# Turning all four tiles of a far pair by DMA instead of two on TensorE

## What is computed

```python
Wh = h @ W.T
sim = Wh @ Wh.T / (norms * norms.T + EPS)
mask = (adj > 0) | eye
alpha = softmax(where(mask, sim, -inf), axis=1)
x = layernorm(x + alpha @ Wh)
agg = mask2 @ x / max(deg, 1)                 # mask2 = adj > 0
y = relu(concat([x @ W_self + b_self, agg @ W_nb + b_nb]) @ W_comb + b_comb)
out = layernorm(x + y)
```

## Time and profile before

| | us |
|---|---|
| median of 3 runs (lowest, highest) | 878.36 (876.25, 879.7) |
| the profiled execution, its own time | 876.79 |
| its span in the profile | 875.0 |
| PE busy / DVE busy / ACT busy in the span | 855.9 / 585.5 / 374.8 |

### The profile page before, as it was taken

The page is one execution under the profiler, slowest core; times in us unless marked ns, Lnnn a source line. Parts: engine busy times, 40 slices in busy tenths (PEclk is TensorE's granted clock), DMA queues, the critical chain, the costliest instruction groups (busy, mean ns, idle before and its releaser), DMA issues.

```text
span 875.0 us, 18251 instructions
## 1 busy us (share of the span) xinstructions
PE 855.9 (98%) x6871; PEld 685.3 (78%) x6871; DVE 585.5 (67%) x1336; ACT 374.8 (43%) x619; POOL 66.5 (8%) x177
## 2 busy tenths in 40 slices
PE   8999999999999999999999999989999999999997
PEld 6867777777777777777777777768888888888886
DVE  2777887879767797778878878889525333333333
ACT  4867656656556565555656556554210000000000
POOL 2400000000000000000000000011101110001101
PEclk9999999999999999999999999999999999999999
DMA  7997685567777777798879699865753303321300
GB/s 201 276 218 193 178 220 151 151 169 209 188 175 213 206 206 191 179 229 209 209 201 232 181 221 318 207 173 140 201 89 133 115 19 109 115 87 47 115 19 19
DMA packets 209566, 146.89 MB, mean 168 GB/s; under 512 B 123473, under 2 KB 187234, under 8 KB 208450
## 3 DMA queue, kind: packets, MB, share of 16 engines
q1 hardware_dynamic: 209282, 145.28, 62.1%
q0 software_dynamic: 192, 0.41, 0.2%
HBM read 95.83 MB, written 28.85 MB: 142 GB/s over the span
## 4 chain that ended last, share of the span: by engine, by line
issue 81%; PE 10%; POOL 5%; DVE 2%; ACT 1%; POOLq 1%; DMA 0%; DVEq 0%; SPq 0%; ACTq 0%
PE ps L1355 3%; POOL rstd L656 3%; POOL var_eps L654 2%; PE ps L1446 1%; PE ps L1448 1%; PE ps L1447 1%; PE ps L1386 1%; PE ps L1388 1%; PE ps L1387 1%; ACT mask L724 1%; PE ps L1440 1%; DMA feat<-xT 0%; ACT prob_hi L719 0%; DVE feat L873 0%; DVE work L1025 0%
## 5 line engine op out<-in xcount | busy, mean ns | idle before, releaser
L1446 PE MATMUL ps<-feat,prob_hi 128*128 128x257 f16 x1024 | 280.7, 274 | 4.0 <-DVE prob_lo L1032 3.9
L1448 PE MATMUL ps<-feat,prob_lo 128*128 128x257 f16 x1024 | 279.7, 273 | 0.0
L1447 PE MATMUL ps<-feat,prob_hi 128*128 128x256 f16 x1024 | 278.7, 272 | 0.0
L1635 PE MATMUL ps<-big,mgroup 128*128 128x257 f16 x992 | 219.2, 273 | 0.0
L1636 PE MATMUL ps<-big,mgroup 128*128 128x256 f16 x992 | 219.2, 273 | 0.0
L719 ACT ACTIVATE prob_hi<-work 128x512 f16<-128x512 f32 x172 | 106.6, 628 | 104.4 <-DVE work L992 42.1
L1032 DVE SCALAR_TENSOR_TENSOR prob_lo<-work,prob_hi 128x512 f16<-128x512 f32 x172 | 117.2, 686 | 22.6 <-ACT prob_hi L719 20.9
L1446 PEld LDWEIGHTS ps<-feat,prob_hi 128*128 128x128 f16 x1024 | 99.8, 97 | 30.3 <-DVE prob_lo L1032 5.4
L1447 PEld LDWEIGHTS ps<-feat,prob_hi 128*128 128x128 f16 x1024 | 100.4, 98 | 24.7
L712 ACT ACTIVATE work<-ps 128x512 f32<-128x512 f32 (+2 forms) x144 | 79.2, 552 | 74.2 <-PE ps L1388 70.7
L1448 PEld LDWEIGHTS ps<-feat,prob_lo 128*128 128x128 f16 x1024 | 99.5, 97 | 13.4
(11 more groups left out here) (142 smaller groups left out, 995.6 us busy)
## 6 DMA issues: line engine op xcount, KB each, us to landing
adj_sb<-adjT SPq DMA_DIRECT2D x128, 512.0 KB, 4.5
mask_spill<-mask SPq DMA_DIRECT2D x128, 128.0 KB, 4.0
mgroup<-mask_spill SPq DMA_DIRECT2D x8, 2048.0 KB, 8.0
xres<-x SPq DMA_DIRECT2D x8, 512.0 KB, 5.8
x1h_dram<-big SPq DMA_DIRECT2D x16, 256.0 KB, 5.5
out<-rows SPq DMA_DIRECT2D x32, 128.0 KB, 1.7
feat<-xT SPq DMA_DIRECT2D x7, 512.0 KB, 6.8
unit_dram<-feat SPq DMA_DIRECT2D x7, 512.0 KB, 4.5
```

What stands on the lines that cost most here:

```text
L1446: pe.matmul(acc(D + 1), prob_hi[:, s, cols], feat_hi_of(g)[:, r, 0:D + 1], start=start, stop=False)
L1447: pe.matmul(acc(D), prob_hi[:, s, cols], feat_lo_of(g)[:, r, :], start=False, stop=False)
L1448: return pe.matmul(acc(D + 1), prob_lo[:, s, cols], feat_hi_of(g)[:, r, 0:D + 1], start=False, stop=stop)
L1635: pe.matmul(agg_ps(q, D + 1), lhsT, z_hi_of(g)[:, r, 0:D + 1], start=(jb == 0), stop=False)
```

## The change

For far pairs, all four tiles are turned by DMA. `block_scores` and its eight transposes per pair go, and with them `mask_blocks`, `mask_direct`, `heads` and `tails` in far pairs: every tile now takes the way of `far_parts`. The two transposing loads of a pair are 512 KB each. In SP's order they stand inside the pair whose tiles they turn (after its second mask store) and no longer at the end of the pair before. The turned tiles are no longer stored as half-width strips: the adjacency and the masks of the turned side are loaded and stored in the direct shape. The buffers move into `mgroup[:, 1]`, so that the second group's masks are loaded later. The first group's masks are loaded at step 6 instead of 4. `unitT` and `x1T` are loaded by transposing DMAs straight from SBUF; the DRAM buffers go. The layout of `unitT` becomes block by block, so the moving operand of the score matmuls is four runs of 128 columns.

```diff
-MGROUP0_STEP = 4
+MGROUP0_STEP = 6
@@ SP
             def turn_far(a, b):
                 k = far_before(a) + b - a - 1
-                sync.wait_ge(far_hi_ready, 2 * (k + 1))
-                sync.wait_ge(far_lo_ready, 2 * (k + 1))
+                sync.wait_ge(far_hi_ready, GB * (k + 1))
+                sync.wait_ge(far_lo_ready, GB * (k + 1))
                 for h in range(2):
-                    sync.dma_start_transpose(far_turned(h).rearrange("p r (s i) -> p (r s) i", s=GB),
+                    sync.dma_start_transpose(far_turned[:, h].rearrange("p r (s i) -> p (r s) i", s=GB),
                                              far_parts[:, h].rearrange("p r i -> p (r i)")).then_inc(far_loaded, 16)
             def pair_far(a, b):
                 for m in range(4):
...
-                        store_turned(a, b, 3 - m, slot)
-                if b < G - 1:
-                    turn_far(a, b + 1)
+                        store_direct(b, a, m - 2, slot)
+                    if m == 1:
+                        turn_far(a, b)
-            def store_x1(a):
+            def turn_x1(a):
                 sync.wait_ge(x1_ready, (a + 1) * GB)
                 for h in range(2):
+                    sync.dma_start_transpose(x1T_of(a, h).rearrange("p b k i -> p (b k) i"), x1_half_of(a, h)).then_inc(x1T_loaded[a], 16)
@@ ACT, pair_far
                 def high(r):
                     act.wait_ge(exp_ready, f0 + r + 1)
                     wait(act, far_loaded, 32 * k)
...
-                for r in range(2):
-                    exponentials(t0 + r, c0 + r, f0 + r, r, GB)
+                for r in range(GB):
+                    exponentials(t0 + r, c0 + r, f0 + r, r, GB, 0, GB * (k - 1) + r + 1 if n else None)
                     high(r)
-                unit_kept(u0, 0, 2 * k + 1)
+                    if r in (1, 2):
+                        unit_kept(u0 + r - 1, r - 1, 4 * k + r)
...
@@ DVE, pair_far
+                for r in range(GB):
+                    if r % 2 == 0:
+                        keep_unit(r // 2)
                     damping(a, b * GB + r, c0 + r, f0 + r, r)
...
+                    low(r)
+                    if n:
+                        block_copied(b - 1, r, t0 - GB + r)
+                    masked_parts(t0 + r, r, kept(r // 2)[:, r % 2 * GW:(r % 2 + 1) * GW], far_parts[:, 0, r, :], far_parts[:, 1, r, :], lambda ap: ap)
+                    beside()
+                keep_unit(2)
+                keep_unit(3)
...
                 dve.wait_ge(far_loaded, 32 * (k + 1))
+                for x in range(GB):
+                    masked_parts(t0 + GB + x, x, kept_block(x), halved(far_turned[:, 0, x]), halved(far_turned[:, 1, x]), halved)
+                    beside()
@@ PE
-            def block_scores(r, f):
-                pe.wait_ge(exp_ready, f + 1)
-                for x in range(GB):
-                    ins = pe.transpose(score_ps(r)[:, x * P:(x + 1) * P], expo[:, r, x * P:(x + 1) * P], ident[:, :])
-                ins.then_inc(score_done, 1)
             def pair_far(a, b):
                 for j in range(STEP_TILES):
-                    if j < 2:
-                        front_far(a, b, GB + j)
-                    elif j >= GB and b < G - 1:
+                    if j >= GB and b < G - 1:
                         front_far(a, b + 1, j - GB)
```

More of the change, by code:

```diff
@@ L206, in gnn_program, with kept, kept_block @@
         mixw = rows
[L207 to L216, removed]
+        def kept(m):
+            return prob[:, m, :].bitcast(F16)
+        def kept_block(x):
+            return work[:, 6 * GW:8 * GW].bitcast(F16).rearrange("p (s i) -> p s i", s=GB)[:, :, x * P:(x + 1) * P]
         def halved(ap):
@@ L454, in _ @@
             load_unit(0, 1, 1, 3)
[L455 to L459, removed]
+            for g in range(1, PROMPT - 1):
+                turn_units(g)
             def load_norms(a):
@@ L709, in exponentials @@
                 wait_apart(act, score_done, c + 1, act_passed)
-                wait(act, prob_ready, t - since + 1)
+                if free is None:
+                    wait(act, prob_ready, t - since + 1)
+                else:
+                    act.wait_ge(far_lo_ready, free)
                 act.activation(expo[:, r, first:], score_ps(r)[:, first:], ACT.Exp,
@@ L1149, in pair_far, with beside @@
                 t0, f0, u0 = (first + more for first, more in zip(tiles_before(a), (GB + n * STEP_TILES, GB + n * GB, 2 + n * 4)))
-                c0 = scores_before(a) + GB + n * 6
-                h0 = heads_before(a) + GB + n * GB
+                c0 = scores_before(a) + GB + n * GB
                 k = far_before(a) + n
-                loaded = lambda m: 16 * ((u0 + m) // 4 + 1)
+                share = -(-len(between) // (G - b))
+                places = iter(range(1, STEP_TILES + 2))
+                def beside():
+                    place = next(places)
+                    for _ in range(place * share // (STEP_TILES + 1) - (place - 1) * share // (STEP_TILES + 1)):
+                        if between:
+                            between.pop(0)()
@@ L1159, in low @@
                                              op0=ALU.mult, op1=ALU.subtract).then_inc(far_lo_ready, 1)
-                def beside(count=1):
-                    for _ in range(count if between else 0):
-                        if between:
-                            between.pop(0)()
-                more = 2 if a == G - 2 else 1
-                for r in range(2):
-                    damping(a, b * GB + r, c0 + r, f0 + r, r)
-                low(0)
-                low(1)
-                keep(u0, 0, t0)
```

243 lines of the change are left out of this document (85 added, 158 removed).

## The result

| | median us | lowest, highest | over before |
|---|---|---|---|
| before | 878.68 | 876.25, 879.70 | |
| after | 942.47 | 940.94, 944.01 | 1.073 [1.0701, 1.0759] |

The change makes the kernel 7.3% slower. The forecast was 934 with a range of 897 to 960.

What follows compares the result with a forecast made beforehand. PE, busy for 98% of rows 1 to 6, was taken to bound the kernel. 876.8 - 21 (work removed) + 64 (waits for turned tiles) + 14 (VectorE's loop) = 934 us, range 897 to 960.

Steps and rivals of the forecast that it cites:

- transposes removed: PE, rows 1 to 6: 168 transposes in 42 groups of 0.43 us go, 18.1 us less.
- PE's small waits before, gone: Idle time of PE or its weight load ahead of the transposes, 6.8 us in all; 3 taken as saved.
- waits for the turned tiles: PE stands in each far pair of rows 1 to 6 until both transposing loads land: 64 us in sum.
- VectorE's loop: VectorE's work from landing to landing, 17.7 us against PE's 18.1; norm work on it adds 14 us, 0 to 30.
- clock behind the waits: Rival: PE's idle gaps bring 1.2 GHz back, 11 x 2.6 = 29 us, time 961, chance 0.08; not in the sum.
- T: Time for both 512 KB transposing loads of a far pair: 7.3 us taken, range 6 to 8.
- the chain: From the end of a pair's fourth tile's scores through exp, parts, loads and first masked tile: 2.9 + 7.3 = 10.2 us.
- The first rival: Transposing loads cost their issue, not their bytes: 4.5 us for both, wait hidden, time 867, chance 0.08.
- The second: Rival: transposing loads run at the plain rate, 4.8 us for both, time 880, no change to tell, chance 0.06.
- The cover: PE's other work while the turned tiles come: 7.9 us in middle pairs, 6.6 in first and last, 5.3 in row 6.
- The other edits: Direct-shaped loads and stores, `unitT` and `x1T` without DRAM, four-run score operands: costed at nothing.
- The signs that the forecast named: Stage of rows 1 to 6 470 to 480 us, PE busy around 395, 21 low-part waits, loads issued in 2.5 us.

Runs made afterwards that it cites:

- third experiment: All norm pieces of a far pair put at one place, just ahead of VectorE's wait for the landing, against the changed kernel: 941.5 us, 1.0714 of before.
- PE's work put back: Eight transposes with unused results added to every far pair, against the kernel that turns each pair's tiles in two halves: 870.76 us, 0.992 of before.
- two steps: Changed kernel with each pair's tiles 0 and 1 loaded as soon as ready, tiles 2 and 3 after, four 256 KB loads: 860.47 us, 0.9803 of before.

## Why the prediction was nearly right, step by step

The stage sum in the forecast's own terms, in us:

| step | forecast | measured |
|---|---|---|
| transposes removed | -18 | -18.1 |
| PE's small waits before, gone | -3 | -10 |
| waits for the turned tiles | +64 | +66.6 |
| VectorE's loop | +14 | 0 |
| clock behind the waits | 0 | +27.0 |
| sum | +57 | +65.5 |

**Removed: right for the work, too small for the waits.** The 21 waits for turned tiles make 66.6 of the 68.1 us of idle time, so 1.5 is left of the 11.5 that stood there before, and 10 went with the change, not 3. I had read the 6.8 us ahead of L1474 and missed the other small waits of the stage. That they go because PE's long stand in each pair gives everything else slack is my reading; no run shows it.

**T and the chain: right.** 7.3 taken, 6.85 measured in the pair shown and 7.2 in the mean of all; the chain 10.2 taken, 9.7 measured in the pair shown. Both ways to T in the forecast (four small loads in a row, and bytes at 210 GB/s) held: the new loads flow at 205 to 214 GB/s with the DMA share at 1.12 to 1.14. The first rival, a cost for each load and not for its size, would have had T at 4.5; it is refuted by 6.85, and by the 2.3 us of issue for 512 KB against 1.3 for 256 KB. The second, transposes at the plain rate, is refuted by the same 6.85 and by the 205 to 214 GB/s. By the Trainium skill ("Advanced Engine Details and Errata", X-Bar Transpose) T would have been 4.8 (the prediction's estimate from its 350 to 400 GB/s). The traces here do not agree with it, at 6.85.

**The cover: right, pair by pair.**

| pairs | forecast, each | measured, mean (lowest to highest) |
|---|---|---|
| 10 middle ones | 2.3 | 2.5 (2.0 to 3.3) |
| 5 first ones of a row | 3.6 | 3.6 (3.4 to 4.4) |
| 5 last ones | 3.6 | 3.7 (3.3 to 4.4) |
| row 6 | 4.9 | 5.2 |

**VectorE's loop: wrong.** This is the step where I took 14 of 0 to 30. Moving all of the pieces to where VectorE stands idle (third experiment) changed the time by 1 us, inside the noise. VectorE's loop was counted at 17.7 us and PE's at 18.1, and I took near equality as a cost. Why it was none is argued from the trace and not tried: the chain to the loads starts with PE's scores, for which ScalarE waits (198.1 us in 103 places), so the pieces ahead of it lie mostly in time that PE's order leaves free.

**The clock: this is the step that failed by most.** It stood among the rivals with 0.08 and not in the sum. The forecast itself had PE standing for 3.6 to 5 us in eleven places, and the only ground for no loss was that PE kept 1.00 before, when its longest wait in the stretch was 1.4 us. That says nothing of what long waits do. Measured were 27.0 us, against the rival's 29, but made up in another way: not eleven waits by 2.6 but sixteen by 1.4 to 2.9. In order of length, the 21 waits and what the matmuls behind them took too long:

```
wait  2.00 2.01 2.02 2.02 | 2.31 2.51 2.74 3.06 3.08 3.30 3.33 3.33 3.35 3.36 3.36 3.38 3.53 3.98 4.35 4.37 5.22
slow  0    0    0    0    | 1.7  1.7  1.4  1.7  1.7  1.6  0    1.6  1.5  1.4  1.6  1.7  1.7  1.7  2.9  1.7  1.6
```

Each costs less than the 2.6 of the rival because the clock is back before the block and the score tile are done: in the windows above, 0.50, then 0.77, then 1.00. The Trainium skill ("TensorE: Matmul & The Clock Gate", Why this matters for your kernels; the prediction names the section otherwise) warned of just this, that idle gaps between bursts of matmuls bring the lower clock back. The trace agrees: 16 of the 17 longer waits are followed by it.

**The two errors offset.** 14 too much for VectorE and 7 too little for small waits gone are 21 too much; 27 for the clock and 2.6 for longer waits are about 30 missing. Together 8.5, the distance from 934 to 942.5. The sum was nearer than its terms: that 934 lies within 1% of the result is luck, that PE would stand in each of the 21 pairs, and for how long, is not. Two sums of the rivals were off by 2 us without bearing on the forecast: 934 + 29 is 963 and not 961, and the second rival's 13 + 10 is 23 and not 25.

**The other edits: not nothing.** They were costed at 0. With PE's work put back, two steps are 6.6 us faster than before, so these edits and the new order of VectorE's work give some us. In the changed kernel itself this can't be seen behind the long waits.

**The signs that the forecast named** came as told where the chain was concerned: 21 waits for the low part, the loads issued in 2.3 us (2.5 told) with the second landing after 4.7 (4.6 told), no transposes. The stage was to last 470 to 480 us and lasted 485. PE busy was to be 395 and is 420.8: less the 27.0 of slow matmuls that is 394. VectorE's wait for the landing is there, but under the name "issue".

## What to carry to other kernels

Before work is moved from a busy engine to DMA, the whole way from the last input to the first use has to be set against the work that the busy engine has in that time; here 9.7 us against the 7.9 counted decided, not the 18 us of work saved. A batch of loads waits for its last member: the same bytes in two steps turned +7.3% into -2.0%. Where a forecast makes TensorE stand for long, again and again (here 16 of 17 waits of 2.3 us and more were followed by the lower clock, and none of the four of 2.0), the clock belongs in the sum. A mean clock under 1.00 in a windows' row, or a busy time that rises though work was taken away, was the sign of it here (0.94, and 7.7 us more).

## What was unexpected of the hardware

- The granted clock fell to 0.50 behind waits of only 2.3 to 2.7 us, though not behind one of 3.33, nor behind four of 2.0. Each fall cost some 1.4 to 1.7 us (once 2.9).
- Matmuls that nobody needs, 336 of them for 37 us, made the changed kernel 14 us faster.
- The issue of a transposing load holds SP for longer the more bytes it has: 1.24 to 1.34 us for 256 KB, 2.32 for 512 KB, in the medians.
- With turning loads in two steps the DMA share was 1.02 over 200 us, and PE still had work for 99% of that time.
